# Query stage of a fused two-layer kernel: weights stored transposed, head norms summed and spread in groups of the array, small steps between the products

## The reference, cut to what matters

```python
q = _causal_conv1d(_causal_conv1d(q, qc1_w, qc1_b, N_HEADS), qc2_w, qc2_b, 1)   # 1024 channels, 3 taps
q = q.reshape(B, S, N_HEADS, HEAD_DIM) + 0.5 * k_mean[:, :, None, :]            # 16 heads of 64
k = k.reshape(B, S, N_KV, HEAD_DIM) + 0.5 * q_mean[:, :, None, :]               # 4 heads of 64
q = _l2norm(q)                                  # x / max(sqrt(sum of squares over a head), 1e-12)
k = _l2norm(k) * key_temp
q = _rope(q, cos, sin)                          # neighbouring channels turned by a position's angle
k = _rope(k, cos, sin)
```

## Time and profile before

| | us |
|---|---|
| median of 3 runs | 2966.08 |
| the three runs | 2960.21, 2966.08, 2969.19 |
| the profiled execution | 2957.02 |
| its span, first to last instruction | 2955.1 |
| mean granted TensorE clock | 0.935 |
| query stage, first transfer issued to first of the next stage | 760.6 to 1462.5 |
| first product of tile 0, last product of tile 7 | 794.6 to 1411.2 |

### The profile page before, as it was taken

One profiled execution on the slowest core, in us unless ns is written; L12 is line 12 of the kernel. 1 busy time (PEld: TensorE's weight loads), 2 busy tenths in 40 slices (PEclk: granted clock), 3 DMA queues, 4 the chain that ended last, 5 costly groups with the idle time before them and its releaser, 6 DMA issues. The chain is left out here.

```text
span 2955.1 us, 31069 instructions
## 1 busy us (share of the span) xinstructions
PE 2541.4 (86%) x11893; PEld 1202.7 (41%) x11954; DVE 1249.0 (42%) x2633; ACT 947.3 (32%) x1601; POOL 794.4 (27%) x747
## 2 busy tenths in 40 slices
PE   7999669999697999999399997788658888888866
PEld 3444334444354555555233333344323333333323
DVE  2332241111322322321156774244577778777712
ACT  1111120101211111110166662022326767667640
POOL 0111101111333333333333431022343333333300
PEclk9999889999798999999699998899769999999988
DMA  5000010000221010100222212431285445554222
GB/s 206 29 29 29 29 50 32 32 14 10 90 48 53 15 58 15 57 15 20 84 86 79 79 47 107 142 119 59 88 167 71 59 61 64 72 70 64 34 74 103
DMA packets 132259, 189.28 MB, mean 64 GB/s; under 512 B 45000, under 2 KB 67144, under 8 KB 130704
## 3 DMA queue, kind: packets, MB, share of 16 engines
q1 hardware_dynamic: 130000, 183.11, 24.6%
q10 hardware_dynamic: 2112, 4.19, 0.4%
HBM read 126.97 MB, written 60.29 MB: 63 GB/s over the span
## 5 line engine op out<-in xcount | busy, mean ns | idle before, releaser
L877 PE MATMUL c_ps_c<-conv_in,c_wT 128*128 128x512 f16 x2304 | 510.7, 383 | 1.5 <-DVE c_wT L1026 1.5
L2153 ACT ACTIVATE f_probs<-f_ps_s 128x512 f32<-128x512 f32 x576 | 320.5, 596 | 145.1 <-PE f_ps_s L2059 61.4
L2271 DVE TENSOR_REDUCE f_chunk_max<-f_ps_a 128x64 f32<-128x1024 f32 x320 | 321.2, 1033 | 96.3 <-PE f_ps_a L2030 52.6
L877 PEld LDWEIGHTS c_ps_c<-conv_in,c_wT 128*128 128x128 f16 x2304 | 226.4, 98 | 276.6 <-issue 11.2
L2059 PE MATMUL f_ps_s<-f_qs,f_ks 128*128 128x512 bf16 x576 | 213.0, 389 | 58.1 <-ACT f_probs L2153 50.3
L1271 ACT ACTIVATE d_probs<-d_ps_s,d_shift 128x512 f32<-128x512 f32 (+3 forms) x384 | 196.3, 583 | 111.5 <-PE d_ps_s L1210 110.5
L2030 PE MATMUL f_ps_a<-f_ka,f_qa 128*128 128x512 bf16 (+3 forms) x707 | 183.9, 339 | 50.4 <-DMA f_v_all<-v 21.9
L968 POOL TENSOR_TENSOR c_rnorm<-c_norm,half 128x32 f32<-128x32 f32 x10 | 54.5, 5453 | 470.1 <-DVE c_norm L1031 470.1
L1001 DVE SCALAR_TENSOR_TENSOR c_raw<-c_ps_c,c_w_unscale,c_offset 128x512 f32<-128x512 f32 x32 | 24.0, 751 | 362.1 <-PE c_ps_c L877 362.1
L2079 PE MATMUL f_ps_o<-f_probs,f_v 128*32 128x512 f32 (+3 forms) x1536 | 154.7, 498 | 25.6 <-ACT f_probs L2153 25.4
L624 PE MATMUL b_ps<-b_xb,b_wT 128*128 128x512 f32 x320 | 139.6, 597 | 17.9 <-DMA b_xb<-xnT 17.9
(11 more groups left out here) (272 smaller groups left out, 3862.8 us busy)
## 6 DMA issues: line engine op xcount, KB each, us to landing
f_qa<-qk SPq DMA_DIRECT2D x96, 128.0 KB, 3.9
f_qs<-qk SPq DMA_DIRECT2D x96, 128.0 KB, 5.0
d_q<-q_parts SPq DMA_DIRECT2D x8, 1024.0 KB, 5.3
o0T<-d_stage SPq DMA_DIRECT2D x16, 512.0 KB, 2.6
e_o_in<-o0T SPq DMA_DIRECT2D x4, 2048.0 KB, 10.4
qk<-e_part SPq DMA_DIRECT2D x12, 640.0 KB, 4.9
rows<-in_qc_w SPq DMA_DIRECT2D x4, 1536.0 KB, 9.1
c_rows<-in_qc_w SPq DMA_DIRECT2D x4, 1536.0 KB, 11.5
```

What stands on the lines that cost most here:

```text
L877: last = pe.matmul(ps_c[n % 2][:], wT[u][:, w, i * TAPS + a, :], conv_in[:, x, i, b, h * CH + a:h * CH + a + CH], start=(i == 0 and a == 0 ...
L2153: act.activation(probs[m % HELD][:, :, at:at + P], ps_s[n % 2][:].rearrange("p (h n) -> p h n", n=P), ACT.Exp, scale=HD1 ** -0.5).then_inc ...
L2271: dve.tensor_reduce(chunk_max[:, qt - 2, :, at:at + w // CHUNK], src.rearrange("p h (c k) -> p h c k", k=CHUNK), AX.X, ALU.max).then_inc(a ...
```

## The change

All of it is in the query stage and in the constants and input layouts that it reads.

**Weights.** The input array of the second convolution is laid out so that a tile's rows have input channels on the partitions and, within them, 24 blocks of 128 output channels. The 24 transposes per tile, their two banks, and the scaling of the rows in place are gone. A scale per output channel would now lie along the free axis, so there is one scale for the whole tile: VectorE takes each partition's largest and smallest value (`extremes`), TensorE turns that column into one row (`find_peak`, one product of 128 columns), VectorE takes the largest (`tallest`), TensorE puts it on all partitions (`share_peak`, one product of 1 column), and VectorE makes the scale and its inverse (`scales`). ScalarE and VectorE make the high and low parts straight from the loaded rows, in four pieces of 768 columns each (`weights`, `lows`). Products of chunk 0 wait piece by piece.

**Sums and spread.** The head sums have `head_sum` (128 x 32, two columns of it used) as weights and 512 tokens as data, and the four chunks go to partitions 0, 32, 64 and 96 of one bank, `ps_n`. ScalarE copies the bank (`sums_out`), TensorE transposes it in four blocks (`turn`), VectorE floors 128 x 32 values (`norms`), GpSimd takes the power and writes the factor into `strips` (`invert`, 128 x 32 values and no longer 128 x 2048), TensorE transposes back (`back`), ScalarE copies (`rnorms`), and the spread is four products of 512 columns, each with 32 partitions of `head_spread` as weights and 32 partitions of `strip_t` as data, into four banks `ps_b`.

**Places.** A hook stands behind every 36 products, two to a chunk. For a tile m of 1 to 6: hook 0 has `find_peak` of tile m + 1, hook 1 the sums of unit m + 1 and `share_peak`, hooks 2, 3 and 4 have turn, back and spread. Tile 0 has the four steps of unit 0 at hooks 0 to 3 and those of unit 1 at hooks 4 to 7, besides the two for the peak. The rows of tile 1 are loaded ahead of the tables, and the tables are seven.

The core of the difference:

```diff
-
-
-        def after(m, n):
+        def source(j):
+            return k_in if j == 0 else raw[1] if j == 1 else raw[(j - MK) % 2]
+
+        def hook(m, h):
+
+            todo = []
             if m == 0:
-                return ((("spread", 0), ("turn", 0)), (("turn", 1), ("sums", 1)), (("turn", 2),), (("spread", 1),))[n]
-            turn = () if m == MQ - 1 else (("turn", n),)
-            return ((("sums", m + 1),) + turn, turn, (("spread", m + 1),) + turn, ())[n]
+                j, step = divmod(h, 4)
+                todo.append((("sums", "turn", "back", "spread")[step], j))
+            elif 1 <= h <= 4:
+                todo.append((("sums", "turn", "back", "spread")[h - 1], m + 1))
+            if m + 1 < MQ and h < 2:
+                todo.append((("peak", "scale")[h], m + 1))
+            return todo
...
             for j, to in enumerate((k_in, raw[1])):
                 sp.dma_start(to[:], dram["k_raw"][j]).then_inc(k_loaded, 16)
+            load_rows(1)
             sp.dma_start(k_mean[:], dram["k_mean"]).then_inc(tables, 16)
...
-            sp.dma_start(head2[:], dram["head2"]).then_inc(tables, 16)
+            sp.dma_start(head_sum[:], dram["head_sum"]).then_inc(tables, 16)
+            sp.dma_start(head_spread[:], dram["head_spread"]).then_inc(tables, 16)
...
-            def turn(k, u, groups):
-
-                for g in groups:
-                    if g == 0:
-                        pe.wait_ge(w_scaled, k + 1)
-                    if g >= 2 or k > 0:
-                        pe.wait_ge(w_ready, WG * k + g - 1 if g >= 2 else WG * k)
-                    for j in range(4):
-                        i, a = divmod(4 * g + j, TAPS)
-                        last = pe.transpose(ps_t[g % 2][:, j * P:(j + 1) * P], rows[u][:, i * P:(i + 1) * P, a], ident[:])
-                    last.then_inc(w_turned, 1)
-
             def sums(j):
 
                 pe.wait_ge(square_ready, j + 1)
                 if j > 0:
-                    pe.wait_ge(norm_ready, j)
-                for t in range(T // P):
-                    last = pe.matmul(ps_s[:, 2 * t:2 * t + 2], square[:, t * P:(t + 1) * P], head2[:], start=True, stop=True)
+                    pe.wait_ge(rnorm_ready, j)
+                for n in range(NCH):
+                    last = pe.matmul(ps_n[n * STRIP:(n + 1) * STRIP, :], head_sum[:], square[:, n * CH:(n + 1) * CH], start=True, stop=True)
                 last.then_inc(sums_done, 1)
 
+            def turn(j):
+
+                pe.wait_ge(sums_ready, j + 1)
+                for b in range(BLK):
+                    last = pe.transpose(ps_n[:, b * P:(b + 1) * P], strip_t[:, b * P:(b + 1) * P], ident[:])
+                last.then_inc(turned_done, 1)
+
+            def back(j):
+
+                pe.wait_ge(strips_ready, j + 1)
+                for b in range(BLK):
+                    last = pe.transpose(ps_n[:, b * P:(b + 1) * P], strips[:, b, :, :].rearrange("p n k -> p (n k)"), ident[:])
+                last.then_inc(back_done, 1)
+
             def spread(j):
 
                 pe.wait_ge(rnorm_ready, j + 1)
+                if j > 0:
+                    pe.wait_ge(unit_ready, NCH * j)
                 for n in range(NCH):
+                    strip = slice(n * STRIP, (n + 1) * STRIP)
+                    pe.matmul(ps_b[n][:], head_spread[strip, :], strip_t[strip, :], start=True, stop=True).then_inc(spread_done, 1)
+
+            def find_peak(k):
+
+                pe.wait_ge(w_step, W_STEPS * k + 3)
+                pe.matmul(ps_x[0:1, 0:P], ends[:, 2:3], ident[:], start=True, stop=True).then_inc(peak_done, 1)
+
+            def share_peak(k):
+
+                pe.wait_ge(w_step, W_STEPS * k + 4)
+                pe.matmul(ps_x[:, P:P + 1], ones[:], peak[:], start=True, stop=True).then_inc(peak_done, 1)
+
+            steps = {"sums": sums, "turn": turn, "back": back, "spread": spread, "peak": find_peak, "scale": share_peak}
+
...
+                        if n == 0 and i % 2 == 0:
+                            pe.wait_ge(w_ready, PIECES * m + i // 2 + 1)
...
-                    last.then_inc(conv_done, 1)
-                    for what, j in after(m, n):
-                        if what == "sums":
-                            sums(j)
-                        elif what == "spread":
-                            spread(j)
-                        else:
-                            turn(m + 1, 1 - u, range(2 * j, 2 * j + 2))
+                        if i == MQ - 1:
+                            last.then_inc(conv_done, 1)
+                        if i % 4 == 3:
+                            for what, j in hook(m, 2 * n + i // 4):
+                                steps[what](j)
...
-            def scale_rows(k, u):
-
-                act.wait_ge(w_step, 5 * (k + 1))
-                act.activation(rows[u][:].rearrange("p i a -> p (i a)"), rows[u][:].rearrange("p i a -> p (i a)"), ACT.Identity,
-                               scale=w_scale[u][:, 0:1]).then_inc(w_scaled, 1)
+            def weights(k):
+
+                act.wait_ge(w_step, W_STEPS * (k + 1))
+                if k >= 2:
+                    act.wait_ge(conv_done, NCH * (k - 1))
+                for x in range(PIECES):
+                    act.activation(wT[k % 2][:, 0, x * PER:(x + 1) * PER, :], rows[k % 2][:, x * PER:(x + 1) * PER, :], ACT.Identity,
+                                   scale=w_scale[k % 2][:, 0:1]).then_inc(w_high, 1)
...
+            def sums_out(j):
+                act.wait_ge(sums_done, j + 1)
+                act.activation(strip_t[:], ps_n[:], ACT.Copy).then_inc(sums_ready, 1)
+
+            def rnorms(j):
+                act.wait_ge(back_done, j + 1)
+                if j > 0:
                     act.wait_ge(spread_done, NCH * j)
-                act.activation(square[:], src, ACT.Square).then_inc(square_ready, 1)
+                act.activation(strip_t[:], ps_n[:], ACT.Copy).then_inc(rnorm_ready, 1)
```

More of the change, by code:

```diff
@@ L901, in _ @@
+            pe.wait_ge(tables, 16 * 7)
+            pe.wait_ge(cleared, 2)
+            find_peak(0)
+            share_peak(0)
+            for m in range(MQ):
+                tile(m)
+            for what in ("sums", "turn", "back", "spread"):
+                steps[what](UNITS - 1)
         @block.scalar
         def _(act):
-            def weights(k, u, groups):
-                for g in groups:
-                    act.wait_ge(w_turned, WG * k + g + 1)
-                    act.activation(wT[u][:, 0, 4 * g:4 * g + 4, :].rearrange("p j n -> p (j n)"), ps_t[g % 2][:], ACT.Copy)\
-                       .then_inc(w_high, 1)
@@ L919, in squares @@
+            def squares(j):
                 if j < MK:
@@ new lines, in _ @@
+            sums_out(0)
+            offsets(1)
+            weights(1)
+            rnorms(0)
+            squares(1)
+            highs(0)
+            sums_out(1)
+            rnorms(1)
+            highs(1)
+            for m in range(1, MQ):
+                squares(m + 1)
+                if m + 1 < MQ:
+                    offsets(m + 1)
+                sums_out(m + 1)
+                if m + 1 < MQ:
+                    weights(m + 1)
+                rnorms(m + 1)
+                highs(m + 1)
@@ L1084, in _ @@
-            tile(MQ - 3, 1, MQ // 2)
-            tile(MQ - 2, 0, None)
-            tile(LAST, 1, None)
-            norms(MQ + 1, raw[1][:])
-            split(MQ + 1)
+                dve.tensor_tensor(low[:], turned[:].rearrange("p b s -> p (b s)"), high[:], ALU.subtract).then_inc(low_ready, 1)
+            extremes(0)
+            tallest(0)
+            scales(0)
+            lows(0)
+            shuffle(0)
+            extremes(1)
+            tallest(1)
+            take(0, 0)
+            norms(0)
```

324 lines of the change are left out of this document (157 added, 167 removed).

## The result

| | before | after |
|---|---|---|
| median, runs of the same session | 2967.26 us (2960.21 to 2969.19) | 2876.31 us (2871.49 to 2878.54) |
| ratio of the runs, 95% interval | | 0.9695 (0.9675 to 0.9716) |
| the profiled execution, its span | 2957.02, 2955.1 | 2878.54, 2876.7 |
| mean granted TensorE clock | 0.935 | 0.938 |
| query stage, first transfer to first of the next | 701.8 us | 615.5 us |

What follows compares the result with a forecast made beforehand. TensorE was taken to set the query stage's length. Product stretch 71.3, start 4.3 and end 11.1 sum to 86.7 us less; 2966.1 - 86.7 = 2879 us, range 2858 to 2906.

Steps and rivals of the forecast that it cites:

- steps between them: Between TensorE's products: nine units of sums, turn, back and spread at 3.08, seven peak pairs at 0.6: 31.9 us.
- stand in tile 0, in tile 1: TensorE waiting at hook 0 for VectorE's extremes of the next tile: 1.7 us in tile 0, 9.4 in tile 1.
- lower level: TensorE's products at the lower clock: 2.1 us more at the stage's start, 2.1 after the stand in tile 1.
- Row groups: Spread's four products on 32 array rows each: taken to run all at once, 1.08 us, with 3.54 as upper bound.
- The serial rival: Spread's four row-group products run one after the other, 3.54 us each spread: 22 us more, 2901; chance 0.12.
- GpSimd's chain: Hooks 2 to 3: 6.8 us against 8.2, no wait; rival: late every tile, up to 51 us, likelier 2905, chance 0.10.
- The clock: Rival: TensorE's clock falls at the 42 hooks, up to 2.11 us each, 89 us; 2968 to 2990, chance 0.05.
- The drain: TensorE's array changing shape at the new steps: 0.08 us on the way in, already in the sum.
- the longer drain: Array shape changes costing 0.16 us in and out at 32 groups: 10 us, the sum some 6 longer.
- The start: Query stage's start: tables' wait ends 4.2 us later, steps behind it 10.7, first product at 790.3, 4.3 earlier.
- The end: Query stage's end, last take to last low part: 33.4 us in place of 44.5, 11.1 less.

Runs made afterwards that it cites:

- the three edits: Changed kernel with tile 2's extremes earlier, tables before tile 1's rows, and the last unit's exchange and rotation by halves: 2850.16 us, ratio 0.9616.

## Why the prediction was right

| term | forecast | measured |
|---|---|---|
| 2304 products at the full level | 498.2 | 498.6 (64 blocks of 7.79) |
| steps between them | 31.9 | 33.4 (what is left of 547.8) |
| stand in tile 0, in tile 1 | 1.7, 9.4 | 1.9, 9.0 |
| lower level | 2.1 + 2.1 | 1.5 + 1.7 + 1.6 |
| first product to last take | 545.4 | 547.8 |
| first product earlier by | 4.3 | 5.1 |
| end, last take to last low part | 33.4 | 32.2 |
| the stage shorter by | 86.7 | 86.3 |

The mechanism held: what stood between the products went, and no new wait came but the two forecast. That the sum came within 0.4 us is luck in part. The stretch of products was 2.4 us longer than forecast, and the start and the end were 0.8 and 1.2 better. That the median came within 3 us of 2879 is no closer than the runs of one kernel, which lie 7 to 9 us apart.

The split between the parts is less sure than the whole. The old form of the sums costs 40 us in the changed kernel, and the new weights give 29 in the kernel before, by runs. Which of the two had more of the 86 us isn't shown, as the number of chunks at the lower level changes with what stands beside the sums. The old spread was never put into the changed kernel; by the rows, 3.79 against 1.08, 0.09 ahead and 0.44 for the transposition back, its new form gives about 2.2 us a unit, 20 us for nine (an estimate).

*Row groups.* The choice was 1.08 by the earlier trace rows, its 0.08 ahead included. Measured so it is 1.08 + 0.09 = 1.17, where four on the whole array one after the other are 3.44. So the groups do run beside each other, and the term was 0.8 us too small over nine units. The serial rival would have cost 17.3 in the stage, not 22. The Trainium skill (TensorE: Matmul & The Clock Gate, Measured speedup vs the span model) gives 3.07 times for this packing; here it is 3.44 / 1.08 = 3.2 between starts, and 3.44 / 1.17 = 2.9 with the time ahead, so this trace agrees within what can be told here.

*GpSimd's chain.* The forecast of no wait held, with 0.8 us to spare and not 1.4. The narrow write was 0.29 to 0.37 as taken. The power was the surprise:

```profile
902.96 6.17 POOL L1007 TENSOR_TENSOR c_rnorm<-c_norm,half 128x32 f32<-128x32 f32 x1 [3.50 <-DVE c_norm L1080]
```

It is 6.16 to 6.17 in tiles 1 to 6, where VectorE's low parts of the weights run beside it, and 5.45 in the four others, so its mean is 5.88. In the run with the power twice the first of a tile took 6.16, beside the low parts, and the second, behind them, 5.43. The forecast named VectorE's steps on two operands as a danger and put them at nothing in the sum. They took half of the slack, and doubling the power showed how little was left.

*The clock.* From 888 us on it is at its full level through all hooks, so that rival is out. The lower level came in three blocks of tiles 0 and 1, one more than forecast.

*The drain.* It is 0.09 ahead of sums and spread, and the sum had 0.08 of that, so the longer drain is out too. By the forecast's own figures its price was too low: 10.2 less the 1.4 that the sum had is 8.8 us, not 6.

*The start* came 0.8 earlier than forecast. The tables' wait was 3.0 later than before and not 4.2, and the steps behind it took 11.1 and not 10.7. The run with the tables first gives 3.1 us of wait back, so the rows ahead of the tables are what made it later.

*The end* was 1.2 us shorter than forecast, most of it in the last sums: they took 1.06, where 2.0 was taken for the lower level. That was luck: behind the same stand of 2.79 they took 1.94 in the runs of the three edits and of the early extremes, and 1.06 in the changed kernel run again.

## What to carry to other kernels

Where one engine sets a stage's length, list the gaps between its blocks and price each new step by its own start-to-start time; here that gave 86.7 us for 86.3, with parts that were off by up to 2.4 and cancelled. Count then, engine by engine, when each hand-over is ready against when it is asked for in the first tiles, since the steady tile hides those stands: one line moved in VectorE's order was worth 9.5 us. And a part's cost is not what its instructions take: in a steady tile the old sums took 4.2 us themselves and held up the products behind them by another 2.4.

## What the runs showed of the hardware

- Sixteen fp32 products with 2 columns as data take 3.5 to 3.6 us at the full level, up to 4.8 where part of them runs at the lower one, and 7.0 where all do. The next chunk of 72 then holds products at the lower level in every tile of both runs that kept them (in tiles 1 to 7, 16.9 to 18.6 us in place of 15.74). In the kernel before it did so in tiles 0, 1, 3, 4 and 6, and in tiles 2, 5 and 7 the next chunk was no longer than elsewhere. So these products often bring the lower level and not always, and what decides it was not tried. Spreads of 3.44 us (four fp32 products with 512 columns) and 3.8 us (sixteen with 128) didn't bring it in any tile of the kernel before or of the run with the spread on the whole array.
- Stands of TensorE of 1.28 to 1.55 us at the peak in tile 0 left the next block at 7.96 (four runs), and those of 1.85 to 1.97 at 9.64 (four runs). In the run with the power twice a stand of 3.92 left it at 7.94, and one of 3.93 in tile 7 at 9.94. The length alone doesn't decide it, and what does was not tried.
- SyncE's issue of a 64 KB table took 7.1 to 7.4 us behind 4.5 MB of transfers in its queue, in all seven runs with that order, where the other issues at the stage's start took 0.3 to 0.7. With the 1.5 MB of rows behind the tables the longest was 2.9 to 3.1. A transfer put first delays the issue, and not only the landing, of those behind it: the last table was issued 11.5 us after the stage's first transfer, and 7.4 with the tables first.
- GpSimd's power on 128 x 32 values takes 5.45 us, and 6.17 beside three-operand steps of VectorE in SBUF.
- Four fp32 products with 512 columns on 32 rows of the array each took 1.08 us, and four on the whole array 3.44. The 16-bit products ahead of the four groups took 0.09 us longer, and nothing more could be seen behind them.
